# Attention of a graph network in steps of one edge row with a node block each (832 gathers in place of 856), with sums in three PSUM banks and one bank for turned weights

## The reference

```python
x_l = (x @ W_l).reshape(n, H, C)
x_r = (x @ W_r).reshape(n, H, C)
e = (ea @ W_e).reshape(-1, H, C)
m = jax.nn.leaky_relu(x_l[src] + x_r[dst] + e, NEG_SLOPE)
alpha = jnp.einsum('ehc,hc->eh', m, att)
amax = jax.ops.segment_max(alpha, dst, num_segments=n)
expa = jnp.exp(alpha - amax[dst])
denom = jax.ops.segment_sum(expa, dst, num_segments=n)
a = expa / (denom[dst] + 1e-16)
out = jax.ops.segment_sum(x_l[src] * a[:, :, None], dst, num_segments=n)
```

## Time and profile before

| what | before |
|---|---|
| median of 3 runs | 2233.2 us (2232.06 to 2237.89) |
| the profiled execution: its own time | 2248.54 us |
| its span, from the first to the last instruction | 2246.7 us |
| mean granted PE clock, as a share of full speed | 0.864 |
| busy: PE, DVE, ACT, POOL | 1820.9, 1327.8, 1066.6, 847.4 us |
| first and last gather of the attention | 846.3 us and 2125.6 us |

### The profile page before, as it was taken

One profiled execution on the slowest core, in us unless ns is written; L12 is line 12 of the kernel. 1 busy time (PEld: TensorE's weight loads), 2 busy tenths in 40 slices (PEclk: granted clock), 3 DMA queues, 4 the chain that ended last, 5 costly groups with the idle time before them and its releaser, 6 DMA issues. The chain is left out here.

```text
span 2246.7 us, 35285 instructions
## 1 busy us (share of the span) xinstructions
PE 1820.9 (81%) x10692; PEld 1277.1 (57%) x10692; DVE 1327.8 (59%) x3113; ACT 1066.6 (47%) x2345; POOL 847.4 (38%) x891
## 2 busy tenths in 40 slices
PE   6777799979999973677878878878888778888776
PEld 2667665567888741345545555545555545555564
DVE  6999777664333363755555555555555555555585
ACT  1889867545423450234434444434444444444465
POOL 2000000010000016766666666666666666666500
PEclk9555599989999996799898998888989998999887
DMA  3000000005300012323233223323233233323311
GB/s 104 24 2 1 8 2 1 5 25 151 91 1 6 1 44 69 90 77 82 77 80 83 78 80 82 82 76 84 77 81 81 77 81 82 83 76 82 79 35 29
DMA packets 132195, 133.01 MB, mean 59 GB/s; under 512 B 28888, under 2 KB 102063, under 8 KB 132015
## 3 DMA queue, kind: packets, MB, share of 16 engines
q1 hardware_dynamic: 104238, 73.55, 11.4%
q0 software_dynamic: 27776, 57.20, 10.3%
HBM read 125.84 MB, written 4.82 MB: 58 GB/s over the span
## 5 line engine op out<-in xcount | busy, mean ns | idle before, releaser
L2275 POOL DMA_INDIRECT rows<-x_l,src x856 | 821.3, 959 | 477.1 <-issue 224.3
L2400 ACT ACTIVATE bent<-psum 128x512 f32<-128x512 f32 x214 | 127.4, 596 | 606.6 <-DMA near<-e_ends 340.6
L2361 PE MATMUL psum<-both,node_hot 128*128 128x144 f32 x1712 | 308.6, 323 | 66.3 <-issue 56.0
L2361 PEld LDWEIGHTS psum<-both,node_hot 128*128 128x128 f32 x1712 | 265.9, 213 | 143.0 <-issue 127.2
L2548 DVE TENSOR_TENSOR acc<-acc,psum 128x144 f32 x428 | 127.0, 297 | 278.4 <-remote 198.3
L2293 PEld LDWEIGHTS psum<-hot,x_r_parts 128*128 x1284 | 133.5, 104 | 249.0 <-issue 228.6
L2293 PE MATMUL psum<-hot,x_r_parts 128*128 128x256 bf16 x1284 | 201.2, 296 | 90.3 <-DVE hot L2454 31.1
L2415 ACT ACTIVATE apart<-iota,rel 128x128 bf16<-128x128 f32 x856 | 270.6, 388 | 1.4 <-PE psum L2361 1.4
L2313 PE MATMUL psum<-bent,att_heads 128*128 128x512 f32 x428 | 244.7, 661 | 9.0 <-DVE bent L2458 6.1
L2296 PE MATMUL psum<-edges,w_e 128*128 128x512 f32 x428 | 239.5, 642 | 0.7 <-issue 0.7
L2458 DVE TENSOR_TENSOR bent<-psum,bent 128x512 f32<-128x512 f32 x214 | 146.9, 686 | 127.9 <-issue 117.8
(11 more groups left out here) (347 smaller groups left out, 2400.3 us busy)
## 6 DMA issues: line engine op xcount, KB each, us to landing
rel_row<-e_rel_rows SPq DMA_DIRECT2D x107, 256.0 KB
edges<-edge_t SPq DMA_DIRECT2D x428, 32.0 KB
rows<-x_l,src POOLq DMA_INDIRECT x856
edge_part<-edge_t SPq DMA_DIRECT2D x40, 320.0 KB, 3.1
new<-e_new_before SPq DMA_DIRECT2D x26, 64.0 KB
new<-e_new_behind SPq DMA_DIRECT2D x26, 64.0 KB
ht<-x SPq DMA_DIRECT2D x6, 256.0 KB, 2.8
x_l<-rows SPq DMA_DIRECT2D x4, 320.0 KB
```

Source lines behind the costliest of these rows:

```text
L2275: e.indirect_dma_start(rows[:, g % ring, j * ROW:(j + 1) * ROW], None, k.xl, bass.IndirectOffsetOnAxis(ap=src[:, at:at + 1], axis=0)).then ...
L2361: final = e.matmul(to, near_hot[:, at, j, :], both[:, at, j, :], start=j % 2 == 0, stop=j % 2 == 1)
```

## The change

One row with one node block is now a step: 806 + 24 = 830 steps, four to a group, which makes 208 groups (26 full batches), 832 gathers, and a table of 832 steps in seven chunks of 128. What follows from it:

- `begin` has twelve matmuls of 128 columns in place of six of 256, each with its own block's register; the same number of columns.
- Each row's sum stands by itself. Three banks hold three rows each; a bank is given back when its three rows are added. DVE makes one add per row (four per group in the mean, in lumps of 3, 3 and 6), and PE waits for the adds of the trio nine rows back before it begins a bank anew.
- The weights are turned into one bank in place of two, after the batch before (not the one before that) has been used up.
- The factor at a batch's start is multiplied with 8 heads' values spread over 16 features (two multiplies on DVE in place of one of 136 columns); a mask goes.
- The edges are loaded with four transfers for a group in place of two, and the three engines that use registers load them twice as often.
- The tables: three chunks are found first, then the destinations' work goes on, then the other four; the count for a chunk runs over the range of rows that it can hold only, with a base that POOL writes. There are 14 gathers of half the width in place of 8, and 21 stores of `e_rel_rows` and `e_new_*` in place of 12.

```diff
-        self.groups = -(-(self.pairs + self.nb - 1) // 2)
+        self.groups = -(-(self.tiles + self.nb - 1) // 4)
...
-        groups = Path(k, scope, "e", io["dst_last"], 2, src_pairs, dst_pairs, 7, s.nb, 2 * s.padded)
+        groups = Path(k, scope, "e", io["dst_last"], 1, io["src_rows"], io["dst_rows"], 7, s.nb, 4 * s.padded)
...
+                groups.find(e, v, c, ended, range(3))
                 c.vector_dst(e)
-                groups.vector(e, v, c, ended)
+                groups.find(e, v, c, ended, range(3, en))
+                groups.vector(e, v, c)
...
-        z_banks, sum_banks = (k.bank[0], k.bank[1]), (k.bank[6], k.bank[7])
+        z_banks, sum_banks = (k.bank[0], k.bank[1]), (k.bank[5], k.bank[6], k.bank[7])
...
-            return k.bank[4 + b.two]
+            return k.bank[4]
...
-                    for j, at in enumerate(two):
-                        e.dma_start(edges[0:DE, g % edge_slots, j * 2 * P:(j + 1) * 2 * P].rearrange("d (t e) -> d t e", t=2),
-                                    rows_of_pair(at)).then_inc(*edge_here[g % edge_slots].up(16))
+                    for j, at in enumerate(four):
+                        e.dma_start(edges[0:DE, g % edge_slots, j * P:(j + 1) * P],
+                                    rows_t[bass.ds(at, 1), :, :].rearrange("o d e -> d (o e)")).then_inc(*edge_here[g % edge_slots].up(16))
...
-                    for j in range(2):
-                        half = slice(j * 2 * P, (j + 1) * 2 * P)
+                    for j in range(4):
+                        quarter = slice(j * P, (j + 1) * P)
                         for q in range(3):
-                            e.matmul(z[:, half], row_parts.parts[:, bass.ds(blocks[j], 1), q, :].rearrange("p o f -> p (o f)"),
-                                     hot[:, two, half], start=j + q == 0, stop=False)
+                            e.matmul(z[:, quarter], row_parts.parts[:, bass.ds(blocks[j], 1), q, :].rearrange("p o f -> p (o f)"),
+                                     hot[:, two, quarter], start=j + q == 0, stop=False)
...
-                    if b.i >= 2:
-                        e.wait_ge(weighted.sem, weighted.at(plan[b.i - 2].over))
-                        e.wait_ge(filled.sem, filled.at(plan[b.i - 2].over))
+                    if b.i:
+                        e.wait_ge(weighted.sem, weighted.at(plan[b.i - 1].over))
+                        e.wait_ge(filled.sem, filled.at(plan[b.i - 1].over))
...
-                        to = bank[:, j // 2 * wide:(j // 2 + 1) * wide]
-                        final = e.matmul(to, near_hot[:, at, j, :], both[:, at, j, :], start=j % 2 == 0, stop=j % 2 == 1)
+                        row = 4 * u + j
+                        m, third = divmod(row, 3)
+                        bank = sum_banks[m % 3]
+                        if m >= 3 and third == 0:
+                            e.wait_ge(added.sem, added.at(adds(3 * m - 7)))
...
+                        final = e.matmul(bank[:, third * wide:(third + 1) * wide], near_hot[:, at, j, :], both[:, at, j, :],
+                                         start=True, stop=True)
...
-                    for j, to in enumerate(blocks):
-                        e.wait_ge(added.sem, added.at(adds(u) - 2 + j))
-                        e.tensor_tensor(to, to, bank[:, j * wide:(j + 1) * wide], ALU.add).then_inc(*added.up())
+                    for m in trios(u):
+                        bank = sum_banks[m % 3]
+                        e.wait_ge(totals.sem, totals.at(u + 1))
+                        for row in range(3 * m, min(3 * m + 3, 4 * groups)):
...
+                            e.wait_ge(added.sem, added.at(adds(row) - 1))
+                            e.tensor_tensor(to, to, bank[:, row % 3 * wide:(row % 3 + 1) * wide], ALU.add).then_inc(*added.up())
```

More of the change, by code:

```diff
@@ L206, in vector, with open_tiles, bases @@
         e.wait_ge(v.sem, v.at(t))
+    def open_tiles(self, c):
+        return max(0, c * P - self.windows + 1), min(self.tiles, c * P + P - 1)
+    def bases(self, e):
+        for c in range(self.nch):
+            e.memset(self.base[:, c:c + 1], float(self.open_tiles(c)[0])).then_inc(*self.based.up())
     def gpsimd(self, e):
@@ L495, in tables @@
     s, io = k.s, k.io
-    wide = 2 * P
+    wide = P
     k.ident = k.sb(k.ctx, "ident", [P, P])
@@ L537, in tables @@
         new_ready, stored = k.flag("new_ready"), k.flag("stored")
-        turns = [(srct, 0, srcf), (relt, 0, rel), (srct, 1, srcf), (relt, 1, rel)]
-        assert steps <= 512 and len(c_cuts(s)) == 4
+        turns = [(srct, 0, 4, srcf), (relt, 0, 4, rel), (srct, 4, en, srcf), (relt, 4, en, rel)]
+        assert 4 < en <= 8 and len(c_cuts(s)) == 4
         ends_of = [(rowf, pair), (rows3, trio)]
         def turn(e, i):
-            _, j, of = turns[i]
-            for q in range(en):
-                last = e.transpose(k.bank[i][:, q * P:(q + 1) * P], of[:, q, j * P:(j + 1) * P], k.ident[:, :])
+            _, lo, hi, of = turns[i]
+            for q in range(lo, hi):
+                last = e.transpose(k.bank[i][:, (q - lo) * P:(q - lo + 1) * P], of[:, q, :], k.ident[:, :])
             last.then_inc(*turned.up())
         def move(e, i):
-            to, j, _ = turns[i]
+            to, lo, hi, _ = turns[i]
             e.wait_ge(turned.sem, turned.at(i + 1))
-            e.activation(to[:, :, j], k.bank[i][:, 0:steps], ACT.Copy).then_inc(*moved.up())
+            e.activation(to[:, lo * P:hi * P], k.bank[i][:, 0:(hi - lo) * P], ACT.Copy).then_inc(*moved.up())
         def turn_ends(e, i):
@@ L645, in _ @@
                 c.gpsimd(e)
+                groups.bases(e)
                 groups.gpsimd(e)
@@ L2139, in batch_of, with adds, trios @@
         return next(b for b in plan if b.first <= g < b.over)
-    def adds(u):
-        return 2 * (u + 1) + sum(b.first <= u for b in plan)
+    def adds(row):
+        return row + 1 + 2 * sum(4 * b.first <= row for b in plan)
+    def trios(u):
+        return [m for m in range(-(-4 * groups // 3)) if min(3 * m + 2, 4 * groups - 1) // 4 == u]
     def new_rows(b):
@@ L2346, in sum_rows @@
                 def sum_rows(u):
-                    at, bank = u % deep, sum_banks[u % 2]
-                    if u >= 2:
-                        e.wait_ge(added.sem, added.at(adds(u - 2)))
-                    if u in begun:
-                        i = begun[u].i
-                        e.wait_ge(spread.sem, spread.at(3 * i + 3))
-                        e.matmul(bank[:, 2 * wide:2 * wide + scaled], is_first[:, :], factor[:, :], start=True, stop=False)
-                        e.matmul(bank[:, 2 * wide:2 * wide + scaled], others[:, :], ones[:, :],
-                                            start=False, stop=True).then_inc(*factors.up())
+                    at = u % deep
                     e.wait_ge(hot_scalar.sem, hot_scalar.at(u + 1))
@@ L2520, in spread_fall @@
                     e.wait_ge(exps.sem, exps.at(2 * b.i + 2))
-                    e.tensor_scalar(factor[:, :], mask[:, :], fall[:, b.two, 2:3], None, ALU.mult).then_inc(*spread.up())
+                    e.tensor_scalar(factor[:, :], heads, fall[:, b.two, 2:3], None, ALU.mult).then_inc(*spread.up())
                 def weigh(u):
```

115 lines of the change are left out of this document (59 added, 56 removed).

## The result

The changed kernel takes 2244.12 us (median of 6 runs, 2242.39 to 2248.36), the kernel before beside it 2235.85 us (2232.06 to 2237.89): a ratio of 1.0043, 95% interval 1.0028 to 1.0057. It is slower, by 0.43%. The forecast was 2217 us and faster; 2244 lies within the range given, on the side that the forecast did not take.

The account below looks back on a forecast made before the run. The prediction took a cycle of gathers, 5.98 us a group, as the bound. Fewer groups -35.9, loop +10, tail +8, tables +2 sum to -15.9 us: 2217 us as a median, range from a little below 2202 to 2262.

Parts of the forecast that it names:

- Fewer groups: Attention loop: six groups less, 24 gathers at 1.496 us each, saving 35.9 us.
- What paces a group: Attention loop: a cycle of gathers sets 5.98 us a group, while the other engines need less.
- the cover: Steady loop: extra adds and matmuls hide in idle time; even all in series 5.4 us, below 5.98.
- turns that have no such slack: Loop turns with extra adds or a batch's scans: extra work shows, +10 us, bounds 0 and 156.
- The twelve small matmuls: PE's `begin`: six more weight loads and register instructions, taken as 0.3 us a group, expected to be covered.
- The four edge transfers: SP's queue: two more transfers a group, taken as 0; 1.2 us a group if uncovered.
- The tail: After the last gather: 28 more adds with nothing to cover them, +8 us, bounds +3 and +10.5.
- The tables: Table stage before the attention: more stores and gathers, partly covered, +2 us, bounds -2 and +6.
- The single bank of weights: Turning of weights: waiting for the batch before costs 0; 99 us if it came one turn late.
- C: Whole kernel: uncovered parts sum to about the gain, so no change, 2230 us; chance 0.21.
- A: Steady loop: DVE's adds come on the path, slower, 2254 us with 0.3 of them uncovered; chance 0.24.
- B: PE's turn sets the pace, so small matmuls show, 62 to 179 us less 26; 2269 at 0.3; chance 0.11.

Follow-up runs that it names:

- before_208: The kernel before with 208 groups in place of 214, the last 24 edge rows left out: 2218.07 us, 0.9857 of the kernel before.
- before_registers: The kernel before with registers loaded four values at a time in place of eight, on the faster kind of chip: 2039.88 us, 1.0017 of the kernel before.
- before_four_adds: The kernel before with each of its adds made twice, four a group: 2263.85 us, 1.0058 of the kernel before.
- after_again: The changed kernel, unaltered, run once more on the fourth chip: 2263.48 us, 1.0065 of the kernel before.
- before_again: The kernel before, unchanged, run once for a second profile on the first chip: 2247.37 us.
- after_split_ahead_2: The changed kernel with x_r split into its parts one turn earlier on DVE, fourth chip: 2258.95 us, 1.0041 of the kernel before.
- before_early_parts: The kernel before with PE waiting for x_r's parts as early as the changed kernel does: 2250.5 us, 1.0005 of the kernel before.
- before_with_all: The kernel before, 214 groups, with doubled adds, twelve small matmuls, four edge transfers, one weights' bank and the early wait for x_r's parts: 2281.52 us, 1.0147.
- after_split_ahead: The changed kernel with x_r split into its parts one turn earlier on DVE, third chip: 2022.64 us, 0.9923 of the kernel before.

## Why the prediction was wrong, step by step

**Fewer groups, -35.9 us: right.** before_208 measured -32 us, with an interval from -29 to -36.

**What paces a group: wrong on the result's kind of chip.** The forecast said that the pace is a cycle of gathers, that the joint release of the engines is the landing of the gathers in flight, and that other work is covered as long as PE and DVE need less than 5.98 us. The trace of the kernel before shows otherwise. At 1503.58, when POOL is let go, it has issued 440 gathers (110 groups), and at 1503.34 ACT starts its 105th sloped logits. So PE has only just joined the group whose first gather started at 1467.35 us, and the gathers in flight belong to a group five further on. (By this count POOL waits for the join of the group six back, where the description of the kernel and the prediction say five.) The DMA packets of a gather end 2.2 us after its start (median), on both kinds of chip. Between 1200 and 1850 us ACT starts a group's sloped logits 29.7 us (median) after that group's last rows have landed; in after it is 29.8 us. On the faster kind, in before_registers, it is 1.1 us. The views of the gathers say the same. Here are those of before and of before_registers, each with who waited for it:

```profile
L2275 POOL DMA_INDIRECT rows<-x_l,src x856: 938/944/2094, 846.3 to 2125.6; - x172
...
  PEld psum L2302: 3.4, 2
  PE psum L2302: 0.9, 1
```

```profile
L2275 POOL DMA_INDIRECT rows<-x_l,src x856: 940/947/1591, 846.9 to 1930.7; - x172
...
  PEld psum L2302: 211.5, 205
  PE psum L2302: 156.6, 157
```

So gathers set the pace on the faster kind (5.07 us a group, against 4.14 and 4.61 us that PE and DVE need), and there they cover the extra work. On the slower kind the loop of PE, ACT and DVE, which ends in PE's join, sets it: the gathered rows lie ready, POOL has used up its credit and waits for PE's joins. What is added to that loop shows, as far as it stands on its longest path; the matmuls did, the adds in the steady part did not.

Two things stay open. The same loop takes 3.8 to 4.3 us once no gathers run, and 6.0 us while they do; what the gathers take from it is not their data, and no run shows what it is. And the release keeps step with the gathers all the same: in after nine of ten groups between 1200 and 1850 us have it 1.84 to 2.36 us after the last gather's start, about when its packets end (2.1 to 3.2 us). That coincidence is what I took for a wait for the data. PE's own rows do not help, since on the slower kind they are out of step with the other engines: the first row of a join stands anywhere from 0.5 us ahead of the nearest ACT row that needs one to 2.4 us behind it (nine of ten in after), where it is 0.7 us ahead in before_registers.

**The step that failed: the cover.** It is the pace above, and with it the term "turns that have no such slack", +10 us. On the fourth chip that term was (6.15 - 6.00) x 208 = +31 us, three times as much; some 7 us of it are the start below. (The two first profiles give only 0.07 us a group, 14 us, but there the profiled execution of before was itself 0.6% long.) It was not the adds, which I had feared most: before_four_adds leaves the spacing where it was. The twelve small matmuls cost 0.06 us a group and 12 us in all (I had put 0.3 us a group on PE and counted on cover; the size was too large and the cover missing). The Trainium skill's "TensorE: Matmul & The Clock Gate", section "Back-to-back issue gap", led to an estimate of 0.2 us a group for them if PE set the pace; the runs show 0.06. The four edge transfers cost 6 us where I had written 0.

**A start that I did not see.** A group begins four blocks in place of two, so that x_r's parts are needed sooner, while DVE makes each only after the turn's `bend`. In the profile after, DVE's rows show the order:

```profile
860.83 0.69 DVE L2473 TENSOR_TENSOR bent<-psum,bent 128x512 f32<-128x512 f32 x1 [10.71 <-ACT bent L2418]
...
864.26 0.83 DVE L2075 TENSOR_TENSOR x_r_parts<-rows,x_r_parts 128x640 bf16<-128x640 f32 x1
885.31 0.69 DVE L2473 TENSOR_TENSOR bent<-psum,bent 128x512 f32<-128x512 f32 x1 [20.23 <-ACT bent L2418]
```

A stop of some 20 us there is old; what is new is who ends it. The first row is from after's waits, the second from those of before:

```profile
PE psum L2309 <- DVE x_r_parts L2075: 36.4, 4, 20.7
PE psum L2293 <- DVE bent L2458: 28.9, 4, 18.7
```

Not all of that reaches the gathers. The gathers of the eleventh group start 63.8 us after the first gather in after and 64.2 in after_again, but 57.0 in before and 56.7 in before_again: 7 us. With the parts made a turn earlier it is 58.1 us (after_split_ahead_2). That the whole time gains as much is not shown: by the medians it is 4.5 us, and the intervals overlap. The early wait alone (before_early_parts) gives 59.5 us and no longer time; with the other parts (before_with_all) it is 63.8. So it takes another part of the change with it; which one was not singled out.

**The tail, +8 us: right in kind, less than half in size.** It was 140.1 - 120.9 = +19 us. The two more adds a group make 11 to 14 us of it (132.1 in before_four_adds, against 118.0 and 120.9 in two profiles of the old loop; in the changed kernel 138.3 and 140.1, against 124.8 with half of the adds gone). I had taken 10.5 us and then let idle time absorb a part, which it did not. The rest, some 5 us, I put down to the banks of three rows: PE stops within a group, and in the whole span for up to 4 us where the scans stand ahead of the adds. That this is the cause is read from the rows above; no run took it away.

**The tables, +2 us: neither borne out nor refuted.** The stage behind them has its first matmul (L848, now L862) at 53.0 to 56.8 us in six profiles with the old tables and at 55.4 to 58.2 in five with the new ones, 1.7 us later in the mean. By the first gather it can't be told any more: 842.4 to 850.4 us with the old tables, 845.3 to 850.4 with the new.

**The single bank of weights, 0: right.**

The account on a chip like the result's, from ratios of different sets (so an estimate): six groups -32, adds +13, small matmuls +12, edge transfers +6, weights' bank and early wait +3 (neither of the two told from nothing), which is +2 us; measured +10 there and +15 on the fourth chip. Registers add about 3 (from the other kind of chip). What is left, some 5 to 10 us, lies by the table above in the steady part as well as the tail. A part of it can be the late start. For the rest I have the trio of banks with its waits and the lumps of adds, by exclusion; the two multiplies at a batch's start and the tables were not run by themselves either. A version with finer hand-over (each row's place given back by itself) was not run.

Of my rivals, C came nearest in kind: terms that each are small and sum to the gain and a little over, 14 us above its 2230. A's 2254 is nearer by number (10 us), but that is luck: the adds were not on the path of the steady part. B, the small matmuls, was right in kind, a fifth of its 62 us in size.

No version beat the kernel before on both kinds of chip. The changed kernel with x_r's parts made earlier is 0.9923 of before on one kind and 1.0041 on the other.

## What to carry to other kernels

Removing turns from a loop is worth only their share, and what each turn gains in work, however small, is multiplied by all turns: here 2.8% fewer groups were worth 32 us, and 0.15 us a group took 31 back. When engines are let go together, do not conclude from the moment alone what they waited for: count how many turns each has done. An issuer that is five groups ahead waits for the consumer, and then the consumer's work has no cover. A bound that was measured on one chip (4.61 us against 5.0 with half of the gathers) does not hold for a chip on which another engine sets the pace. Price the tail, where nothing covers, at start-to-start spacing with the hand-over between engines, and look at the first turns for anything that is made just in time.

## What the runs showed of the hardware

The same kernel took 2232.8 to 2251.1 us on three chips and 2037.7 and 2037.9 us on two others. The part ahead of the attention is the same (first gather at 846.9 us in before_registers and 846.6 us in before_early_parts). Of the 211.5 us between the spans of these two, 198.8 lie between the first and the last gather and 13 behind the last. The gathers stand 1.27 us apart without any wait of POOL on the faster kind, and 1.48 to 1.50 us with 1 us of waiting a group on the slower. On the faster kind PE is shown waiting for gathered rows. This row is from the waits of after_split_ahead on the third chip:

```profile
PE psum L2318 <- DMA rows<-x_l,src: 104.9, 120, 3.1
```

On the slower kind it is not, and ACT, DVE and POOL are let go together 2 to 3 us after the last gather in flight has started, when the rows that the join needs have lain ready for some 30 us. It is not the gathers' own speed: their packets end 2.2 us after their start on both kinds. Nor is it PE's granted clock alone: from 1200 to 2000 us that was 0.98 in before_with_all and 0.89 in before_early_parts on the same chip, and the one with the higher clock has the longer groups (6.10 and 6.00 us).

Why a chip is of one kind or the other stays open. It turned the sign of a change: 1.0041 and 0.9923 for the same code.
